# An MoE tower on one core: the first shared group inside the last two attention turns, two EQhl buffers, residual adds from four turns ahead, routing tables in pieces

## What is computed

```
h = take(W.T, x)                        # 16 x 256 tokens, W 256 x 50257
h = h + attn(layernorm(h))              # 6 layers
h = h + ffn(layernorm(h))               # 8 experts, top 2, and a shared one

attn, per layer:  a = layernorm(x)*gamma + beta;  q,k,v = a @ w_qkv
   q = softmax(q, axis=1)  (over the 256 tokens);  k = softmax(k, axis=2)
   context = k v^T;  out = q^T context;  x = out @ w_out + b_out + x
ffn:  gates = x @ gate_w;  top 2 of 8;  softmax over the two
   swiglu_e(x) = (silu(x @ w1) * (x @ w2)) @ w3,  hidden 512
   out = sum over the two experts of weight * swiglu_e(x)  +  swiglu_shared(x)
```

## Time and profile before

| | |
|---|---|
| median of three runs | 1443.81 us (1441.55 to 1447.9) |
| profiled execution | 1445.67 us, span 1443.9 us, mean granted clock 0.95 |
| TensorE busy | 1268.4 us, 88% of the span |
| VectorE, ScalarE, GpSimd busy | 1031.5, 841.1, 963.1 us |
| attention, turn 0 to 95 | about 160 to 961 us |
| shared stage | 961 to 1117 us |
| expert pairs | 1117 to 1430 us |

### The profile page before, as it was taken

The page is one execution under the profiler, slowest core; times in us unless marked ns, Lnnn a source line. Parts: engine busy times, 40 slices in busy tenths (PEclk is TensorE's granted clock), DMA queues, the critical chain, the costliest instruction groups (busy, mean ns, idle before and its releaser), DMA issues. The chain is left out here.

```text
span 1443.9 us, 36933 instructions
## 1 busy us (share of the span) xinstructions
PE 1268.4 (88%) x10994; PEld 1058.4 (73%) x10995; DVE 1031.5 (71%) x2647; ACT 841.1 (58%) x2302; POOL 963.1 (67%) x970
## 2 busy tenths in 40 slices
PE   3231798999999999999999999878998999999996
PEld 3221677888888888788888888744554888888885
DVE  2125799999999999999988889766555455545553
ACT  3110677788878878888887777666542233332321
POOL 0728778789888888898898889647652143343433
PEclk8565899999999999999999999998999999999998
DMA  9762555655564455335433445744434344544441
GB/s 337 237 233 57 113 143 134 160 122 126 129 139 88 118 124 119 64 66 116 79 65 66 105 95 97 112 70 123 128 104 145 57 67 59 73 62 68 63 64 14
DMA packets 350563, 156.66 MB, mean 108 GB/s; under 512 B 280714, under 2 KB 334713, under 8 KB 350496
## 3 DMA queue, kind: packets, MB, share of 16 engines
q1 hardware_dynamic: 315168, 116.92, 36.4%
q0 software_dynamic: 21600, 25.34, 10.3%
q10 hardware_dynamic: 13728, 13.63, 2.7%
HBM read 48.68 MB, written 43.16 MB: 64 GB/s over the span
## 5 line engine op out<-in xcount | busy, mean ns | idle before, releaser
L803 PE MATMUL bank<-hT,Wc 128*128 128x256 f16 x2304 | 285.8, 274 | 45.6 <-DMA hT<-hhl 31.8
L803 PEld LDWEIGHTS bank<-hT,Wc 128*128 128x128 f16 x2304 | 226.7, 98 | 73.3 <-issue 46.0
L758 POOL DMA_INDIRECT out_rows<-h0b,payin x78 | 121.4, 1557 | 209.8 <-DVE h0b L1577 178.1
L900 PE MATMUL bank<-xTg,Wall 128*128 128x256 f16 x1872 | 211.0, 273 | 0.0
L900 PEld LDWEIGHTS bank<-xTg,Wall 128*128 x1872 | 182.9, 98 | 21.8 <-issue 0.2
L1177 ACT ACTIVATE silu<-bank 128x512 f32<-128x512 f32 x110 | 65.6, 596 | 187.2 <-PE bank L900 145.0
L652 POOL TENSOR_TENSOR h0b<-h0b,rows 128x512 f32<-128x512 f32 x80 | 101.5, 1269 | 79.7 <-DVE h0b L1318 40.1
L803 PE MATMUL bank<-Wc,MT 128*128 128x256 f16 x1152 | 142.7, 274 | 13.4 <-DVE MT L1359 12.4
L1505 DVE SCALAR_TENSOR_TENSOR gT<-bank,silu 128x512 f32<-128x512 f32 x110 | 76.1, 691 | 105.5 <-ACT silu L1177 94.8
L803 PE MATMUL bank<-khl,eqT 128*128 128x256 f16 x1152 | 141.3, 272 | 5.5 <-DVE khl L1371 0.3
L803 PE MATMUL bank<-Wc,hT 128*128 128x256 f16 x1152 | 142.8, 274 | 0.0
(11 more groups left out here) (170 smaller groups left out, 2674.1 us busy)
## 6 DMA issues: line engine op xcount, KB each, us to landing
Wall<-in_L_tok_W SPq DMA_DIRECT2D x25, 512.0 KB
Wall<-in_L_ffn_ew SPq DMA_DIRECT2D x24, 512.0 KB, 4.1
emb_last<-Wall ACTq DMA_DIRECT2D x20, 512.0 KB
Wc<-Wn SPq DMA_DIRECT2D x40, 128.0 KB, 2.2
Wst<-in_L_attn_w_qkv SPq DMA_DIRECT2D x12, 384.0 KB
h_rows<-Wall SPq DMA_DIRECT2D x8, 512.0 KB
X<-h_rows POOLq DMA_DIRECT2D x8, 512.0 KB, 6.8
out_rows<-X SPq DMA_DIRECT2D x8, 512.0 KB
```

Source lines behind the costliest of these rows:

```text
L758: pool.indirect_dma_start(out=out_rows, out_offset=bass.IndirectOffsetOnAxis(ap=got(j % PAYS, w, 0, i32), axis=0), in_=yout[j % 2][:, w, : ...
L803: last = mm(to, lhs(a, k, o), moving, start=(i == 0 and k == 0), stop=(i == 2 and k == 1))
L900: last = mm(to, cols(a, e, 2 * k + w, (2 * half + c) * P, P), moving, start=(n_ == 0), stop=(n_ == 5))
```

## The change

1. Two `EQhl` buffers; ScalarE waits for the transpose of two items back.
2. `add_h0(g)` waits for `s_xb` (bias added) and not `s_x`, and is issued after turns 76, 78, ... 90. VectorE's `add` of the last 16 items waits for the transfer of its group. `stats_of` waits for adds alone and is cut in halves of two tiles, in turns 89 to 95; only group 7 is left for after.
3. `high` is split into `normed` (ScalarE, halves for groups 0 and 1 after turns 90 to 93, group 2 between the first two silus) and the cast, which for groups 0 to 2 is GpSimd's `taken`, a copy. The two halves of `h0b` are swapped between groups, so group 0 needs not wait for attention.
4. Ups 0 and 1 of group 0 are in turn 94, ups 2 and 3 in turn 95. `turn_x(0)` is in SP's turn 93, ahead of eqT of item 95. After attention, group 1 follows the first gates at once.
5. `tables()` is seven functions, spread over groups 6 and 7. The pads are written from a buffer made later.
6. The last six weight splits run in turns 82 to 87; loads of the last expert are a turn earlier; `unroll` in `item_loop` now says from which turn on the turns are written out. Small buffers move.

```diff
@@ SP
+                if isinstance(t, int) and t == ITEMS - 3:
+                    turn_x(0)
                 if have(t + 2):
                     turn_eq(...)
@@ POOL
-                pool.wait_ge(s_x, ITEMS + (GT // TB) * (g + 1))
+                pool.wait_ge(s_xb, ITEMS - NB + (GT // TB) * (g + 1))
...
+            def taken(g):
+                if g == 0:
+                    for ready in (s_wq, s_wk, s_wv, s_wo):
+                        pool.wait_ge(ready, 32 * DEPTH)
+                    pool.wait_ge(s_xlo, XALL + 1)
+                if g == 2:
+                    pool.wait_ge(s_gate, 1)
+                pool.wait_ge(s_xf, g + 1)
+                pool.tensor_copy(xhl(g % ROWS, 0), h0b[:, 1 - g % 2, :, :]).then_inc(s_taken, 1)
+            item_loop(pool, one, AHEAD + 1, unroll=ITEMS - NB - 4,
+                      between={ITEMS - NB - 4: add_first} | {ITEMS - NB - 4 + 2 * g: partial(add_h0, g) for g in range(1, NG)} |
+                      {ITEMS - 7: partial(root, 0)})
...
-            add_h0(4)
-            root(0)
             root(1)
-            add_h0(5)
+            taken(0)
             low(0)
             root(2)
+            root(3)
+            taken(1)
             low(1)
-            root(3)
-            add_h0(6)
             root(4)
+            root(5)
+            taken(2)
             low(2)
-            add_h0(7)
-            root(5)
+            root(6)
             low(3)
+            root(7)
             scatter_x(0)
-            root(6)
+            pool.memset(padl ...)
             scatter_x(1)
             low(4)
-            root(7)
@@ PE
-                if isinstance(t, int) and t == ITEMS - 1:
+                if isinstance(t, int) and t == ITEMS - 2:
                     pe.wait_ge(s_xT[0], 16 * GT)
                     pe.wait_ge(s_xlo, XALL + 1)
-                    for freed in (s_eqlo, s_vlo):
-                        pe.wait_ge(freed, ITEMS)
+                    pe.wait_ge(s_eqlo, ITEMS)
                     up_shared(0, 0)
+                if isinstance(t, int) and t == ITEMS - 1:
+                    up_shared(0, 2)
...
+                if isinstance(t, int) and t == ITEMS - 2:
+                    pe.wait_ge(s_vlo, ITEMS)
+                    up_shared(0, 1)
                 if isinstance(t, int) and t == ITEMS - 1:
-                    up_shared(0, 1)
+                    up_shared(0, 3)
...
             gates_of(0)
             gates_of(1)
-            up_shared(0, 2)
-            ranks(0)
-            up_shared(0, 3)
-            ranks(1)
-            gates_of(2)
             for g in range(1, NG):
                 up_shared(g, 0)
+                if g == 1:
+                    ranks(0)
                 down_shared(2 * g - 2)
                 up_shared(g, 1)
+                if g == 1:
+                    ranks(1)
                 down_shared(2 * g - 1)
-                if g + 1 < NG:
+                if g == 1:
+                    gates_of(2)
+                elif g + 1 < NG:
                     ranks(g + 1)
                 up_shared(g, 2)
+                if g == 1:
+                    ranks(2)
                 up_shared(g, 3)
@@ ACT
-                    if not (isinstance(u, int) and u < 1):
-                        act.wait_ge(s_eqT[1 - p], landed(u - 1))
+                    wait(act, s_eqT[p], landed(u - 2))
...
+            def first_ups():
+                silu_of(0, 0)
+                normed(2)
+                silu_of(1, 1)
+            item_loop(act, one, 5, between={
+                ITEMS - 6: partial(normed, 0, 0, 2), ITEMS - 5: partial(normed, 0, 2), ITEMS - 4: partial(normed, 1, 0, 2),
+                ITEMS - 3: partial(normed, 1, 2), ITEMS - 2: first_ups})
             high_shared(0, 0)
             high_shared(0, 1)
             silu_of(2, 0)
             high_shared(0, 2)
             silu_of(3, 1)
+            share_exp(0)
             high_shared(0, 3)
+            share_exp(1)
             for g in range(1, NG):
-                if g + 1 < NG:
+                if g > 1 and g + 1 < NG:
                     share_exp(g + 1)
                 silu_of(HC * g, 0)
-                if g + 3 < NG:
+                if g == 1:
+                    normed(3)
+                    high(3)
+                elif g + 3 < NG:
+                    normed(g + 3)
                     high(g + 3)
                 silu_of(HC * g + 1, 1)
                 for c in range(HC):
+                    if g == 1 and c == 2:
+                        share_exp(2)
+                        normed(4)
+                        high(4)
                     if c >= 2:
                         silu_of(HC * g + c, c % 2)
                     high_shared(g, c)
@@ DVE, one(t)
+                if isinstance(t, int) and t == ITEMS - 1:
+                    gated_shared(0, 0)
+                    gated_shared(0, 1)
...
+            last_stats = {ITEMS - 7: (0, 0, 2), ITEMS - 6: (0, 2, 4), ITEMS - 5: (1, 2, 4), ITEMS - 4: (2, 2, 4), ITEMS - 3: (3, 2, 4),
+                          ITEMS - 2: (5, 0, 4), ITEMS - 1: (6, 2, 4)}
+            late_stats = {ITEMS - 5: (1, 0, 2), ITEMS - 4: (2, 0, 2), ITEMS - 3: (3, 0, 2), ITEMS - 2: (4, 0, 4), ITEMS - 1: (6, 0, 2)}
@@ DVE, after attention
+            low_shared(0, 0)
+            low_shared(0, 1)
+            gate_shared(0, 2)
             choose(0)
+            gate_shared(0, 3)
             choose(1)
             stats_of(7)
             for g in range(1, NG):
-                if g + 1 < NG:
+                if g > 1 and g + 1 < NG:
                     choose(g + 1)
                 gated_shared(g, 0)
+                if g == 1:
+                    rank(0)
                 share(2 * g - 2, 0)
+                if g == NG - 1:
+                    pair_experts()
+                    pair_starts()
                 gated_shared(g, 1)
                 low_shared(g, 0)
+                if g == NG - 1:
+                    pair_places()
+                if g == 1:
+                    rank(1)
                 share(2 * g - 1, 1)
                 low_shared(g, 1)
+                if g == 1:
+                    choose(2)
-                if g + 1 < NG:
+                elif g + 1 < NG:
                     rank(g + 1)
-                if g + 1 == NG - 1:
-                    tables()
+                if g == NG - 2:
+                    counts()
+                    pair_counts()
+                if g == NG - 1:
+                    pair_words()
                 gate_shared(g, 2)
+                if g == 1:
+                    rank(2)
+                if g == NG - 2:
+                    ends = pair_ends()
                 gate_shared(g, 3)
+                if g == NG - 2:
+                    pair_bases(ends)
```

More of the change, by code:

```diff
@@ L157, in tower @@
         Wsc = sb("Wsc", [P, WSN], f32, att)
+        hT = [sb(f"hT{i}", [P, 2, TB, KH, P], f16, att) for i in range(2)]
+        EQhl = [sb(f"EQhl{i}", [P, 2, KH, SEQ], f16, att) for i in range(2)]
         Wc = sb("Wc", [P, 2, WL], f16, att)
@@ L217, in tower @@
             xT[i] = sb(f"xT{i}", [P, GT, 2, KH, P], f16, ffn)
-        nmr = sb("nmr", [P, NT], f32, ffn)
+        silu = sb("silu", [P, 2, 2, W2], f32, ffn)
+        gT32 = sb("gT32", [P, 2, 2, W2], f32, ffn)
+        gThl = sb("gThl", [P, 2, 2, HC, W2], f16, ffn)
         xrow[2], xT[2] = sb("xrow2", [P, GT, ROW], f32, ffn), sb("xT2", [P, GT, 2, KH, P], f16, ffn)
@@ L342, in item_loop @@
                     pair(h, CUT)
[L343 to L346, removed]
+                start = (ITEMS - AHEAD - XPER) // 2 - 1
+                if not unroll:
+                    with eng.Fori(4 * half + quarter, start) as h:
+                        pair(h, PLAIN)
                     with eng.Fori(0, XPER // 2) as b:
                         pair(eng.snap(b + start), LAST, eng.snap(b + (XALL - XPER) // 2))
-                else:
-                    for t in range(ITEMS - AHEAD - XPER, ITEMS - AHEAD):
-                        one(t, t % 2, LAST, t + XALL - ITEMS + AHEAD)
+                    with eng.Fori(start + XPER // 2, (ITEMS - AHEAD) // 2) as h:
+                        pair(h, PLAIN)
+                else:
+                    with eng.Fori(4 * half + quarter, (unroll) // 2) as h:
+                        pair(h, PLAIN)
+                    for t in range(unroll, ITEMS - AHEAD):
+                        c = t - 2 * start
+                        chunk_turn = 0 <= c < XPER
+                        one(t, t % 2, LAST if chunk_turn else PLAIN, c + XALL - XPER if chunk_turn else None)
                         hook(t)
@@ L414, in load_expert @@
                     sp.wait_ge(s_xload, 48 * e)
+                if e == 3 and part in (None, 0):
+                    sp.wait_ge(s_pad, 16)
                 for i, w in enumerate((w1, w2)):
@@ L695, in add_first @@
                 add_h0(0)
-            item_loop(pool, one, AHEAD + 1, between={ITEMS - 12: add_first} | {ITEMS - 12 + 2 * g: partial(add_h0, g) for g in range(1, 4)}, unroll=XPER)
             def root(g):
```

(2 more changed lines are left out.)

185 lines of the change are left out of this document (97 added, 88 removed).

## The result

The changed kernel takes 1440.59 us as a median (1438.47 to 1443.59), the kernel before 1444.56 in the same comparison: a ratio of 0.9973, 95% interval 0.9963 to 0.9983, or -4.0 us where -8.1 was forecast. 1440.59 lies in the forecast range, but it is half of the gain. The profiled execution took 1441.28 us, span 1439.5, against 1445.67 and 1443.9.

The account below looks back on a forecast made before the run. TensorE sets the end, but between attention and experts other engines release it, mainly ScalarE and VectorE. Terms -3.3 + 1.0 - 1.5 - 5.7 + 1.4 = -8.1 us: 1437.6 profiled, 1435.7 median, range 1425 to 1443.

Parts of the forecast that it names:

- Part a: Attention turns up to M94: second EQhl buffer, moved copy and split normalise save 3.3 us, between 0.5 and 6.
- M94: Mark: start of the first product of turn 94, at 945.05 us in the kernel before; forecast 3.3 us earlier.
- Part b: M94 to the third up of group 2: +1.0 us, between -8 and +4, with high(4) waiting for group 0's scatters.
- T0: Mark: end of turn 95's output product, 961.46 us in the kernel before; forecast at M94 + 19.0.
- 0.8 us for the port: After T0: VectorE delayed by GpSimd's work on the shared SBUF port, 0.8 us, between 0 and 3.
- Part c: Groups 2 to 6 (1014.02 to 1088.52 us): order unchanged, -1.5 us from a stall that may not come again.
- reserve of 1.0 us: Up to the third up of group 2: 1.0 us for stalls that a walk has none of, between 0 and 3.
- Part d: Tables in groups 6 and 7: splitting the one piece of 31 operations shortens TensorE's wait, -5.7 us.
- Part e: First expert pair: TensorE waits for its gathered rows because row indices come later, +1.4 us, between 0 and 3.
- Rival 2: Only the tables pay: attention turns gain 0.5 us, group 0's xT comes 3 us late; -3.3 us, 1440.5; chance 0.27.

Follow-up runs that it names:

- one_eq: The changed kernel with one EQhl buffer instead of two: 1445.64 us on chip I, ratio 1.0011 to the kernel before.
- tables_whole: The changed kernel with the table operations in one block again: 1446.47 us on chip I, ratio 1.0016 to the kernel before.
- filled: The changed kernel with early pad writes to slot_x during the first attention turns: 1406.46 us on chip II (kernel before 1413.45), ratio 0.9944.

## Why the forecast was half right

Every step but one came out within 1 us in the first comparison.

- **Part a** (-3.3): M94 is 2.8 us earlier, and 3.8 counted from the start of turn 70 (745.39), which itself came 0.9 late. Turn 91 took 10.1 us (10 forecast). By one_eq the second buffer alone is worth 5.1 us of those turns, more than the part's whole sum; without it the changed turns are 1.3 us longer than those of before. So the buffer and something that it pays for were both sized too small, and the runs don't say what the other is. That the sum came out so near is in part luck.
- **Part b** (+1.0): measured +0.9. M94 to T0 is 19.2 (19.0), xT of group 0 waits 0.55 (0.5), and high(4) does wait; the profile names no releaser, but it starts 1.6 us after GpSimd's last scatter of group 0 (991.70, 0.96 us), on ScalarE's timeline:

```profile
994.23 1.06 ACT L1147 ACTIVATE xrow<-h0b 128x1024 f16<-128x1024 f32 x1 [7.59 <-issue]
```

That is T0 + 32.8 (33), and the first up of group 2 follows at T0 + 36.6 (37). The 0.8 us for the port came as well: VectorE's low part at 962.81 took 1.52 us instead of 0.69, beside GpSimd's copy. GpSimd's one-input copy took 1.57 us (1.7). The Trainium skill, "GPSIMD Engine Reference", section "Engine selection", calls such work roughly line-rate; by the measured row it is three quarters of the two-input neighbour's 2.12.
- **Part c** (-1.5) is the step that failed. The prediction took a wait and a half-clock up of the kernel before as its whole hazard there ("3.7 us that may or may not come again. I take 1.5"), all on the side of gain. Measured: +2.6, a miss of 4.1 us, which is the miss of the whole. The old stall was indeed gone, but the third up of group 2 took 7.4 us instead of 2.6, in starved steps, with a granted clock of 0.5 from 1015.0 to 1021.8, and the fourth 3.5. The term that the sum lacks is this hold-up of TensorE beside the scatters. Its rows were in the trace before, gaps of 0.59 to 1.15 us named issue at 1033, 1050, 1068 and 1086, each ending within 1.5 us after a group's last scatter (the first two are shown below); the prediction doesn't name them, and part b's reserve of 1.0 us, for stalls of another kind, is all that could have covered them. Two of them, on TensorE's timeline of the kernel before:

```profile
1033.10 1.14 PE L948 MATMUL bank<-Wall,gThl 128*128 128x256 f16 x9 [0.59 <-issue]
...
1050.54 1.14 PE L948 MATMUL bank<-Wall,gThl 128*128 128x256 f16 x9 [1.15 <-issue]
```
- **Part d** (-5.7): measured -6.0, tables_whole gives 6.2 back, the down behind waits 1.55 (1.7).
- **Part e** (+1.4): the wait is 1.29. That its removal brings nearly nothing was not seen.

Shown: on chips I, III and in the first comparison the changed order has more starved gaps than the old one (6.4 to 11.2 against 4.4 to 4.5), but not on chip V (3.5 against 4.4); on all of them its longest late signals are two to three times as long. Moving high(4) added gaps on chip IV (6.6 to 13.5) and hardly any on III (11.2 to 11.9). In the changed kernel, taking the scatters away or making them plain takes gaps and late signals away on chip IV, and chip II has none to begin with. Argued, not shown: that the old order hides part of the hold-up under TensorE's own waits in the time of the first sixteen scatters, that work put into these waits uncovers it, and that the missing half of the gain went there. It rests on part c of the profiled executions and on filled's ratio on chip II; the rival, that the order costs the same 4 us by something else that differs between chips, would need the kernel before without scatters, and both kernels on a chip like II. Rival 2, "only the tables pay", gave nearly the right number (1440.5) for the wrong reason, by luck: it had part a used up and group 0's xT late, and neither happened.

Not settled: why one chip of five has no such gaps (chip II is also faster in all, 1413 against 1439 to 1446), and what the scatters hold up, TensorE's instructions, its matmuls or its signals. The packets of the instruction queues don't tell the two kinds apart in number (26, and 44 or 45 in the changed kernel and its variants), and in the changed kernel's trace none of them runs between 991 and 1019 us, where the longest broken row lies.

## What to carry to other kernels

Before you fill an engine's idle time, look at what else runs in that time: idle named issue in the trace of before, however short, can be the edge of a cost that idle time had been covering. Price it as a term with its own upper end, not as noise. Look too at waits named remote on the engines that wait for it: they can show a signal that came long after the work it reports. And when a kernel moves by half a per cent, compare on more than one chip: here the changed kernel and its near variants were 0.15 to 0.3% faster on three chips and in the first comparison, and 0.6% on another.

## What the runs showed that was not expected

- TensorE can stand in the middle of a row of matmuls with all operands ready: steps of 0.70 us between weight loads, 3.5 to 13.5 us of gaps in a stage of about 150, beside indirect scatters of 128 rows of 1040 bytes (0.96 us each on GpSimd). In the expert stage, whose code is a loop and beside whose 78 indirect adds TensorE also works, there are no gaps and no late signals: its only idle time from 1120 us on is 0.3 us for VectorE.
- The DMA engines are not full meanwhile: share 0.27 in the starved stretch from 1013 to 1018.4, whose TensorE clock is 0.69:

```profile
1013.00:1018.40 5.40, 3.11 (x8) 0.56 (x7) 0.02 (x1) 0.00 (x0) 4.76 (x4) 0.69 0.27 99
```

- TensorE's neighbours show the late signals as idle named remote: from 938 to 1112 us ScalarE waits 18.9 us so in the changed kernel and 19.9 in the kernel before, and not once in filled on chip II, whose fourteen downs all signal 0.02 us after their modelled ends.
